# Adding the causal mask of a small self-attention on VectorE instead of multiplying it into the score banks on TensorE

## The reference

```
q = (x @ Wq) per head, k = (x @ Wk) per head, v = (x @ Wv) per head      # 64 batches, 16 heads, 32 rows
scores = einsum('bhqd,bhkd->bhqk', q, k)                                  # 32 x 32 for each batch and head
scores = where(k > q, -inf, scores)
attn = softmax(scores * 256 ** -0.5)
x = x + einsum('bhqk,bhkd->bhqd', attn, v) @ Wo + bo
```

## Time and profile before

| | |
|---|---|
| time, median of 3 runs | 543.1 us (543.04 to 544.62) |
| the profiled execution, its own time | 545.09 us |
| its span in the trace | 543.2 us |
| PE busy | 527.3 us (97%) |
| DVE busy | 444.9 us (82%) |
| ACT busy | 208.3 us (38%) |
| chain that ended last | PE 88%, DVE 4% |
| steps 3 to 14, from 337.5 to 497.1 us | 11 rounds, PE busy in all of the time |

### The profile page before, as it was taken

One profiled execution on the slowest core, in us unless ns is written; L12 is line 12 of the kernel. 1 busy time (PEld: TensorE's weight loads), 2 busy tenths in 40 slices (PEclk: granted clock), 3 DMA queues, 4 the chain that ended last, 5 costly groups with the idle time before them and its releaser, 6 DMA issues.

```text
span 543.2 us, 19544 instructions
## 1 busy us (share of the span) xinstructions
PE 527.3 (97%) x8270; PEld 429.4 (79%) x8270; DVE 444.9 (82%) x860; ACT 208.3 (38%) x415; POOL 48.3 (9%) x86
## 2 busy tenths in 40 slices
PE   8999989999999999999998899999999999999996
PEld 7777968898788988889877767777777777787775
DVE  5666978898988899888973589898888888889883
ACT  2232313232332323323343654554544445544232
POOL 6101000000000000000200111111111111101120
PEclk9999989999999999999999999999999999999999
DMA  7983330333102221022220000000000000000001
GB/s 267 385 207 89 97 89 1 96 96 90 49 28 78 78 78 39 39 78 78 78 78 4 2 1 3 10 10 10 10 10 10 10 10 10 10 10 10 13 0 34
DMA packets 25774, 31.09 MB, mean 57 GB/s; under 512 B 14608, under 2 KB 22672, under 8 KB 23696
## 3 DMA queue, kind: packets, MB, share of 16 engines
q1 hardware_dynamic: 25744, 30.68, 17.5%
HBM read 28.57 MB, written 2.10 MB: 56 GB/s over the span
## 4 chain that ended last, share of the span: by engine, by line
PE 88%; DVE 4%; issue 3%; ACT 3%; DMA 1%; SPq 0%; POOL 0%; DVEq 0%; POOLq 0%; ACTq 0%
PE bank L1376 13%; PE bank L488 11%; PE bank L466 11%; PE bank L457 11%; PE bank L513 10%; PE bank L1351 8%; PE bank L1413 5%; PE bank L504 4%; PE bank L1401 3%; ACT x_oT L628 2%; PE bank L1436 2%; PE bank L1422 2%; PE bank L1329 2%; PE bank L1310 1%; PE bank L1370 1%
## 5 line engine op out<-in xcount | busy, mean ns | idle before, releaser
L488 PE MATMUL bank<-xwv,x_xcT 128*128 128x512 f32 x128 | 60.6, 616 | 1.7 <-issue 0.8
L466 PEld LDWEIGHTS bank<-x_xcT,xwk 128*128 128x128 f32 x512 | 59.5, 192 | 2.8 <-DMA xwk<-in_L_xattn_w_k_dram 1.1
L466 PE MATMUL bank<-x_xcT,xwk 128*128 128x128 f32 x512 | 59.9, 275 | 1.7 <-DMA xwk<-in_L_xattn_w_k_dram 0.9
L457 PE MATMUL bank<-x_xcT,xwq 128*128 128x128 f32 x512 | 59.8, 275 | 0.0
L457 PEld LDWEIGHTS bank<-x_xcT,xwq 128*128 128x128 f32 x512 | 58.5, 192 | 0.0
L513 PE MATMUL bank<-xwo,x_oT 128*128 128x256 f32 x256 | 58.0, 380 | 0.0
L513 PEld LDWEIGHTS bank<-xwo,x_oT 128*128 128x128 f32 x256 | 47.4, 190 | 5.8
L644 ACT COPY x_k_blocks<-bank 64x512 f32<-64x512 f32 x32 | 18.6, 580 | 86.0 <-PE bank L466 85.8
L1351 PE MATMUL bank<-wdT,f_hqT 128*128 128x256 f32 x192 | 45.6, 386 | 0.2 <-ACT f_hqT L1654 0.2
L488 PEld LDWEIGHTS bank<-xwv,x_xcT 128*128 128x128 f32 x128 | 24.0, 193 | 27.6 <-issue 24.0
L1376 PE MATMUL bank<-wuT,f_xqT 128*128 128x192 f32 (+1 forms) x128 | 40.6, 460 | 0.0
(11 more groups left out here) (165 smaller groups left out, 952.3 us busy)
## 6 DMA issues: line engine op xcount, KB each, us to landing
x_ctx_slab<-in_ctx_dram SPq DMA_DIRECT2D x16, 1028.0 KB, 4.8
out_dram<-f_out SPq DMA_DIRECT2D x15, 128.0 KB, 1.7
xall<-in_x_dram SPq DMA_DIRECT2D x1, 1280.0 KB, 14.4
x_first_keys<-in_ctx_dram SPq DMA_DIRECT2D x16, 80.0 KB, 5.2
xwk<-in_L_xattn_w_k_dram SPq DMA_DIRECT2D x1, 1024.0 KB, 5.0
xwq<-in_L_xattn_w_q_dram SPq DMA_DIRECT2D x1, 1024.0 KB, 7.1
xwv<-in_L_xattn_w_v_dram SPq DMA_DIRECT2D x1, 1024.0 KB, 9.2
xwo<-in_L_xattn_w_o_dram SPq DMA_DIRECT2D x1, 1024.0 KB, 13.0
```

The lines of the kernel that those rows point to most:

```text
L457: last = nc.tensor.matmul(bank67[:, j // 4, (j % 4) * P:(j % 4 + 1) * P], xwq[:, k, j * P:(j + 1) * P], xcT[:, k, :], start=(k == 0), stop ...
L466: last = nc.tensor.matmul(bank[2 + j // 4][:, (j % 4) * P:(j % 4 + 1) * P], xwk[:, k, j * P:(j + 1) * P], xcT[:, KD + k, :], start=(k == 0 ...
L488: last = nc.tensor.matmul(bank45[:, half, :], xcT[:, KD + k, :], xwv[:, k, half * 512:(half + 1) * 512], start=(k == 0), stop=(k == KD - 1))
```

## The change

The two constant tiles and the two products that open the score banks go. The 16 score products of a step now each open and close their own piece of the bank. A new tile `causal_mask` (128 rows by 32 keys, float32) is built once on GpSimd, in four pieces of 32 rows. On DVE, `mask_scores` reads the banks, adds the mask (the same 32 columns for all 16 heads) and writes `a_s`; `take_max` and `subtract_max` then read `a_s` from SBUF in place of the banks. `take_max` moves behind `add_attention`. The waits for `a_kb` and `a_qT` stand ahead of the first score product, with one more raise of a semaphore that nobody waits for.

```
-                        nc.gpsimd.memset(key_copies[:], 0.0)
-                        step(nc.gpsimd.memset(causal_rows[:], 0.0))
...
+                        step(nc.gpsimd.memset(causal_mask[:], 0.0))
+                        for g in range(BT):
+                            rows = slice(g * SQ, (g + 1) * SQ)
+                            step(nc.gpsimd.affine_select(out=causal_mask[rows, :], in_=causal_mask[rows, :],
+                                                         compare_op=ALU.is_ge, fill=NEG_HUGE, base=0,
+                                                         pattern=[[-1, SQ]], channel_multiplier=1))
+                        pool.sem_inc(s_clear, 1)
...
-                    rest.take_max(0, 0)
-                    rest.subtract_max(0)
+                    dve.wait_ge(s_clear, 4)
+                    rest.mask_scores(0, 0)
+                    rest.take_max()
+                    rest.subtract_max()
...
                 def scores(t, first=2):
                     score_bank = score_banks(first)
-                    for g in range(RG):
-                        if g == 1:
-                            pe.wait_ge(s_a_kb, t + 1)
-                            pe.wait_ge(s_a_qc, t + 1)
-                        nc.tensor.matmul(score_bank[:, g, :], causal_rows[:].rearrange("p b q -> p (b q)"),
-                                         key_copies[:, 0:GH, :].rearrange("p h k -> p (h k)"),
-                                         start=True, stop=False)
+                    pe.wait_ge(s_a_kb, t + 1)
+                    pe.wait_ge(s_a_qc, t + 1)
+                    pe.sem_inc(s_a_begun, 1)
...
-                                    start=False, stop=(j == KD - 1), tile_position=(g * RR, b * SQ))
+                                    start=True, stop=True, tile_position=(g * RR, b * SQ))
...
-                def take_max(t, first=2):
+                def mask_scores(t, first=2):
                     a_step.begin(t)
                     dve.wait_ge(s_a_s, t + 1)
-                    a_step.later(nc.vector.tensor_reduce(a_top, a_scores(first), AX_X, ALU.max))
-
-                def subtract_max(first=2):
+                    a_step.later(nc.vector.tensor_tensor(
+                        by_group(a_s), score_banks(first).rearrange("p g (n k) -> p g n k", k=SQ),
+                        causal_mask[:].unsqueeze(1).unsqueeze(1).to_broadcast([P, RG, GH, SQ]), ALU.add))
+
+                def take_max():
                     a_step.sync()
-                    nc.vector.tensor_tensor(a_s[:].rearrange("p (g n) k -> p g n k", g=RG), a_scores(first),
+                    a_step.later(nc.vector.tensor_reduce(a_top, by_group(a_s), AX_X, ALU.max))
+
+                def subtract_max():
+                    a_step.sync()
+                    nc.vector.tensor_tensor(by_group(a_s), by_group(a_s),
                                             a_top.unsqueeze(3).to_broadcast([P, RG, GH, SQ]),
                                             ALU.subtract).then_inc(s_a_sh, 1)
...
                 def step(t, attend, norm, gated, down):
                     if attend:
-                        take_max(t)
+                        mask_scores(t)
                     if norm:
                         add_attention(t - 1)
                     if attend:
+                        take_max()
                         subtract_max()
```

More of the change, by code:

```diff
@@ L112, in perceiver_layer @@
         key_mask = sb("key_mask", [P, SK])
-        causal_rows = sb("causal_rows", [P, BT, SQ], BF16)
-        key_copies = sb("key_copies", [P, H, SQ], BF16)
+        causal_mask = sb("causal_mask", [P, SQ])
         head_rows = sb("head_rows", [P, HT])
@@ L417, in blanks @@
                             n //= 2
-                    step = Chain(pool, s_const, 8 + HG + 2 + 2 - 1 + (HT // RH).bit_length() - 1)
+                    step = Chain(pool, s_const, 6 + HG + BT + 2 + 2 - 1 + (HT // RH).bit_length() - 1)
                     step.begin(0)
@@ L1178, in perceiver_layer @@
         ActParts = namedtuple("ActParts", "normalise_n copy_xn copy_qk copy_v exp grid_x copy_oT steps last recount settle")
-        DveParts = namedtuple("DveParts", "begin take_max subtract_max turn_exp divide steps")
+        DveParts = namedtuple("DveParts", "begin mask_scores take_max subtract_max turn_exp divide steps")
         def layer():
@@ L1685, in add_out, with by_group @@
                     nc.vector.tensor_tensor(f_out[:], down_bank, tile_of(t), ALU.add).then_inc(s_f_out, 1)
-                def a_scores(first):
-                    return score_banks(first).rearrange("p g (n k) -> p g n k", k=SQ)
+                def by_group(a):
+                    return a[:].rearrange("p (g n) k -> p g n k", g=RG)
                 a_top = a_m[:].rearrange("p (g n) -> p g n", g=RG)
-                def take_max(t, first=2):
+                def mask_scores(t, first=2):
                     a_step.begin(t)
                     dve.wait_ge(s_a_s, t + 1)
-                    a_step.later(nc.vector.tensor_reduce(a_top, a_scores(first), AX_X, ALU.max))
-                def subtract_max(first=2):
+                    a_step.later(nc.vector.tensor_tensor(
+                        by_group(a_s), score_banks(first).rearrange("p g (n k) -> p g n k", k=SQ),
+                        causal_mask[:].unsqueeze(1).unsqueeze(1).to_broadcast([P, RG, GH, SQ]), ALU.add))
+                def take_max():
                     a_step.sync()
-                    nc.vector.tensor_tensor(a_s[:].rearrange("p (g n) k -> p g n k", g=RG), a_scores(first),
+                    a_step.later(nc.vector.tensor_reduce(a_top, by_group(a_s), AX_X, ALU.max))
+                def subtract_max():
+                    a_step.sync()
+                    nc.vector.tensor_tensor(by_group(a_s), by_group(a_s),
                                             a_top.unsqueeze(3).to_broadcast([P, RG, GH, SQ]),
@@ L1894, in begin @@
                         dve.sem_inc(s_f, 2 * F_STEPS)
-                return DveParts(begin, take_max, subtract_max, turn_exp, divide, steps)
+                return DveParts(begin, mask_scores, take_max, subtract_max, turn_exp, divide, steps)
             return sp_parts, pool_parts, pe_parts, act_parts, dve_parts
```

2 lines of the change are left out of this document (1 added, 1 removed).

## The result

The changed kernel takes **546.43 us** (median of 22 runs, 543.37 to 549.16); the kernel before took 543.26 us in the same session (22 runs, 542.25 to 544.66). The ratio is 1.0055, 95% interval 1.0041 to 1.0068: slower by half a per cent, 3.2 us. The forecast was 543.1 us with a range up to 545.3; the result lies above it. The profiled execution takes 547.05 us, its span is 545.3 us.

The account below looks back on a forecast made before the run. PE was taken to bound the loop, DVE's attention chain steps 0, 1, 2 and 15. Terms +1.72 before the loop, -0.05 first loop step, -2.42 eleven rounds, +0.72 step 15 sum to -0.03: 543.1 us, range 541.9 to 545.3.

Parts of the forecast that it names:

- The loop: Loop steps: PE's round falls from 14.51 to 14.29 us, 0.22 less, 2.42 us over 11 rounds; DVE's reserve is used up.
- 0.31 us: Upper bound of PE's saving per step, if the 0.09 us passage to small pieces goes with the products; 0.22 was taken.
- the loop through both engines: Rival: dependence through DVE and PE sets the round, 14.37 us with a 0.26 delay; 543.9 us; chance 0.12.
- The delays outside the loop: Steps 0, 1, 2 and 15: PE waits for DVE, whose added work costs 0.72 us each; steps 1 and 2 save 0.22.
- The clock's rival: PE's clock falls in a longer wait, 1.3 us: once 544.4 (0.08); twice, or once beside another rival, 545.3 to 545.7 (0.08).
- Steps 2 and 3: Step 2: +0.72 less 0.22 us, PE waiting for `a_o`; first loop step: -0.05 us, DVE's wait and overlap against added work.
- Step 15: After the loop, PE's `values` wait for DVE: +0.72 us.
- Step 0: DVE's subtraction and PE's `values` come later, +0.72 us; the saved mask products give nothing there.
- faster: Rival: step 1's 0.96 us gap swallows step 0's delay, DVE pairs overlap, PE's passage goes; 540.6 us, chance 0.10.
- The loop's last `add_out`: Sign expected in the changed profile: the last `add_out` of the loop comes 0.7 us earlier than before.
- a dip between 285 and 330 us: Sign that the prediction is wrong: PE's granted clock dips in this stretch, in the steps before the loop.
- the fall around 70 us: Existing stretch: PE stood still 1.49 us, then 3.4 us at half clock; it gave the price of one fall, 1.3 us.

Follow-up runs that it names:

- e8_loop_no_mask: Kernel before with no mask applied by either engine in loop steps 3 to 14, steps outside unchanged: 540.66 us, ratio 0.9952.
- e2_loop_only: Mask on DVE in the loop only; steps 0, 1, 2 and 15 keep PE's mask products as before: 541.56 us, ratio 0.9960 to the kernel before.
- e11_products_and_delay: Loop as in the kernel before; in steps 0, 1, 2 and 15 PE keeps its mask products and DVE adds a mask too: 549.14 us, ratio 1.0090.
- e3_outside_only: Mask on DVE in steps 0, 1, 2 and 15 only; the loop keeps PE's mask products as before: 548.88 us, ratio 1.0082 to the kernel before.
- e1_after_fill: Changed kernel with idle PE products put into all the waits of steps 0, 1, 2 and 15: 544.81 us, ratio 1.0012 to the kernel before.
- e9_fill_15: Changed kernel with four idle PE products ahead of the waits in step 15 alone: 545.69 us, ratio 1.0019 to the kernel before.
- e12_loop_and_1: Mask on DVE in the loop and step 1; steps 0, 2 and 15 keep PE's products as before: 542.77 us, ratio 0.9968 to the kernel before.
- e4_before_fill: Kernel before with idle PE products (2, 3, 4, 0 and 1) put into its waits: 547.32 us, ratio 1.0055.

## Why the prediction was wrong

*The loop: right.* Masking addition 0.68 us, 0.71 us from the maximum to the subtraction, DVE's wait gone, eleven rounds 2.41 us shorter for 2.42. That 0.22 us and not 0.31 us is what the products cost PE is shown by e8_loop_no_mask (14.29 us with DVE at leisure). PE starts the down product 0.20 us after `raise_h` ends (394.73 to 394.93) without having stood still, so the delay that the loop through both engines needs is at most 0.20 us, and that loop did not decide.

*The delays outside the loop: right in size.* PE's waits grew by 0.68, 0.73, 0.73 and 0.34 us (with another 0.36 now ahead of `turn_h` in step 15). The clock's rival had them growing to 1.5, 1.7 and 2.1 us, with another 0.22 each; they are 1.23, 1.50 and 1.89. Steps 2 and 3 took +0.51 and -0.03 for +0.50 and -0.05. Step 15 is +0.73 where no fall disturbs it, for +0.72. Step 0 brought 0.66 for 0.72, and the gap behind it vanished, which stood under "faster" but seems to be the fall's doing. The loop's last `add_out` was forecast 0.7 us earlier; it is at 498.03 us in both traces, since the 0.29 and 0.47 us ahead of the loop came on top.

*What failed: the sum has no term for PE's clock.* It lets PE's waits grow by 0.72 us in four places and prices only the delay, at full clock. The falls stood in a rival, with a price and a sign (a dip between 285 and 330 us, which came at 291.5), but with a chance of 0.08 for one fall and 0.08 for two, because waits up to 1.16 us had shown none. The price was right: 1.3 us there, 1.33 us at step 15 (45.06 against 43.73), about 1.5 us a fall over the runs; only behind step 0, with the gap gone, it is 0.47 net. The chance and the number were wrong. Every run of the changed kernel had at least one fall, 2.9 on average against 0.45. With the forecast's price that is -0.03 + 2.4 x 1.3 = +3.1, with the runs' 1.5 us +3.6, less up to 0.96 for the vanished gap: +2.1 to +3.6, and +3.2 was measured. The prediction also took the fall around 70 us as a fact of the kernel; it is a matter of the run, present in four of the 14 profiled executions and absent from e2_loop_only's.

*Shown:* that the delay on DVE makes the falls (e11_products_and_delay, e3_outside_only), that most falls go when the waits are filled (e1_after_fill, 0.4 a run for 2.9; e9_fill_15, with one place filled, 2.2), that the loop's gain is 2.4 us and is there in full (e2_loop_only). *Open:* what decides whether a given wait gets a fall in a given run: 1.50 us and 1.89 us had none in the changed kernel and one each in e3_outside_only. The single places add 0.1 to 0.8 falls a run to the loop's 0.6, 1.8 together, and 2.3 come when all are there. The times of the single places add to 3.4 us against 5.2 for all, which their intervals can hold. That the gaps are PE waiting for its code rests on the timing of the q8 packets, and that the fall hid the gap of step 1, on which kernels have which; neither was tried by a run of its own.

## What to carry to other kernels

Here an operation moved from the engine that bounds a pipelined loop to one with a little room gained only in the loop. In the steps that fill and drain the pipeline the other engine was the one waited for, and there the move cost its full duration. Look for this first, and where it is so write the edit for the loop alone, as e2_loop_only does. A wait of TensorE is to be priced with the clock behind it: here 0.7 us more of waiting cost 0.7 and, in many runs, up to another 1.5. When a time varies from run to run in steps, sort the runs by their mean granted clock before comparing.

## What the runs showed of the hardware

- PE's granted clock fell to 0.50 for 3.4 us behind waits of 0.81 to 1.89 us (once for 6.8 us, behind 1.50 us in e3_outside_only; once already within the wait, of 1.89 us in e9_fill_15), while none followed the waits of 0.43 to 1.17 us at the same places in the kernel before and in e2_loop_only. The same wait did and didn't bring a fall: 0.81 us in step 15 in the changed kernel and in e11_products_and_delay, 1.50 us in step 1 in e12_loop_and_1 and in the changed kernel.
- Instructions added to PE's program ahead of a loop moved a gap that no semaphore ends, and each such gap ended 1.2 to 1.6 us after a 16 KB packet of the instruction queue q8. It was 0.41 to 1.61 us in step 1, and 2.6 us appeared in step 15 with 9 or 18 products added before the loop, but not with 4 in step 15, nor with 18 and 4 together. So a few harmless instructions cost about 3 us at another place (e4_before_fill).
- Reading 512 columns from SBUF or PSUM made no difference on DVE: the maximum took 0.67 us from `a_s` and 0.68 from the bank, the subtraction 0.69 and 0.68.
